# Full attention on one core: column scores issued head by head, and the order of a step's work on TensorE changed

## What is computed

```python
scores = jnp.einsum('bhqd,bhkd->bhqk', q, k) / np.float32(np.sqrt(HD))
attn = jax.nn.softmax(scores, axis=-1)
out = jnp.einsum('bhqk,bhkd->bhqd', attn, v)
```

## Time and profile before

| | us |
|---|---|
| median of 3 runs | 4614.77 (4614.61 to 4633.34) |
| profiled execution | 4615.12 |
| its span in the profile | 4613.0 |
| PE busy | 4186.8 (91%) |
| DVE busy | 3628.9 (79%) |
| ACT busy | 2805.2 (61%) |
| mean granted share of the full PE clock | 0.962 |

### The profile page before, as it was taken

How to read it: one execution, slowest core, us unless ns; L and a number is a source line. 1 busy time by engine, 2 the same in 40 slices (tenths; PEclk the granted TensorE clock), 3 DMA queues, 4 the chain that set the end, 5 groups by cost and what they waited for, 6 DMA issues and landing times. The chain is left out here.

```text
span 4613.0 us, 82689 instructions
## 1 busy us (share of the span) xinstructions
PE 4186.8 (91%) x27418; PEld 2681.1 (58%) x27418; DVE 3628.9 (79%) x8000; ACT 2805.2 (61%) x6209; POOL 1631.0 (35%) x2408
## 2 busy tenths in 40 slices
PE   5959999999999976599999996999799999987998
PEld 2523333333333334377777775888577777766887
DVE  6679999999999949688888884555688888875665
ACT  1428888888888860366767673444467676763343
POOL 2400000000000004465555653444465656554555
PEclk8969999999999998799999997999899999998999
DMA  5943243333343317300000001211200000003221
GB/s 193 374 88 58 48 63 57 49 63 56 49 63 57 49 61 238 100 27 24 27 24 27 24 19 55 57 47 42 60 24 27 24 27 24 27 13 87 84 69 54
DMA packets 368556, 295.67 MB, mean 64 GB/s; under 512 B 66364, under 2 KB 325432, under 8 KB 368192
## 3 DMA queue, kind: packets, MB, share of 16 engines
q1 hardware_dynamic: 368192, 291.11, 25.6%
HBM read 178.74 MB, written 111.21 MB: 63 GB/s over the span
## 5 line engine op out<-in xcount | busy, mean ns | idle before, releaser
L885 ACT ACTIVATE fa_P<-fa_pS 128x512 f32<-128x512 f32 x2048 | 1111.7, 595 | 317.0 <-PE fa_pS L811 267.2
L912 DVE TENSOR_REDUCE fa_mx<-fa_pR 128x2 f32<-128x1024 f32 x1024 | 1206.0, 1221 | 92.6 <-PE fa_pR L792 78.3
L1507 POOL TENSOR_TENSOR wa_pn<-wa_pr,wa_ri 128x512 f32<-128x512 f32 x512 | 700.7, 1369 | 521.7 <-DVE wa_ri L1563 520.8
L1443 ACT ACTIVATE wa_pr<-wa_sm,wa_mn 128x256 f32<-128x256 f32 x1024 | 510.6, 502 | 172.2 <-DVE wa_mn L1555 172.2
L1136 POOL TENSOR_TENSOR ao_xn<-ao_xn,ao_mod 128x1024 f32<-128x1024 f32 x16 | 37.5, 2347 | 1585.9 <-DVE ao_xn L1101 1585.9
L826 PE MATMUL fa_pO<-fa_P,fa_V 128*32 128x512 f32 x4096 | 546.4, 605 | 0.2 <-ACT fa_P L885 0.2
L811 PE MATMUL fa_pS<-fa_Q,fa_K 50*128 50x512 f32 x2048 | 507.5, 492 | 41.3 <-ACT fa_P L885 11.0
L811 PEld LDWEIGHTS fa_pS<-fa_Q,fa_K 50*128 50x128 f32 x2048 | 191.2, 183 | 517.1 <-ACT fa_P L885 431.3
L792 PE MATMUL fa_pR<-fa_K,fa_Q 48*128 48x512 f32 x2048 | 430.7, 463 | 57.3 <-DMA fa_K<-parts_d 38.3
L1295 PE MATMUL wa_pQK<-wa_wqkv,wa_xT 128*128 128x512 f32 x1536 | 420.0, 409 | 4.7 <-DVE wa_qa L1600 4.7
L1555 DVE CUSTOM_DVE_ANT_0 wa_sm<-wa_pS,wa_mask 128x256 f32<-128x256 f32 x1024 | 374.1, 420 | 18.5 <-issue 11.6
(11 more groups left out here) (188 smaller groups left out, 7156.6 us busy)
## 6 DMA issues: line engine op xcount, KB each, us to landing
parts_d<-pj_parts SPq DMA_DIRECT2D x64, 512.0 KB, 5.4
fa_Q<-parts_d SPq DMA_DIRECT2D x192, 128.0 KB, 4.4
fa_K<-parts_d SPq DMA_DIRECT2D x192, 128.0 KB, 7.4
v_d<-pj_v SPq DMA_DIRECT2D x16, 1024.0 KB, 8.2
fa_V<-v_d SPq DMA_DIRECT2D x32, 512.0 KB, 9.7
pj_x<-in_L_attn_x SPq DMA_DIRECT2D x16, 512.0 KB, 7.6
fa_Q<-fa_nrow SPq DMA_DIRECT2D x512, 2.0 KB
att_d<-fa_att SPq DMA_DIRECT2D x64, 128.0 KB, 2.0
```

The source lines that it names most:

```text
L885: nc.scalar.activation(Pr[:, k % 2, h, :], pS[:, (s * exped.per + u) % T, :], ACT.Exp).then_inc(exped.sem, 1)
L912: nc.vector.tensor_reduce(mx[:, q // QB, :, a, q % QB, kh], row_slot(), AX.X, ALU.max).then_inc(row_free, 1)
L1443: last = nc.scalar.activation(pr[:, hp % 2, hh, :], sm[:, hp % 2, hh, :], ACT.Exp, bias=mn[:, p, h:h + 1], scale=-1.0, accum_out=rs[:, p, ...
L1507: nc.gpsimd.tensor_tensor(pn[:, hp % 2], pr[:, hp % 2], inv, ALU.mult).then_inc(s["weighted"].sem, 1)
```

## The change

`scores` takes a head instead of a pair. It issues one matmul and has a wait of its own, on the exponential three heads earlier. The steps of TensorE's `body` are in another order: head 0, head 1, first row pair, head 2, value batch of the step before, head 3, second row pair, and then the turn where there is one. The number of matmuls, their shapes, the three banks and the two slots stay as they were. TensorE has two more waits for each step.

```diff
-                def scores(n, s, k, a):
+                def scores(n, s, k, h):
                     half, kb = k // KB, k % KB
-                    u = k * GH + 2 * a
-                    if kb == 0 and a == 0:
+                    u, a, at = k * GH + h, h // 2, h % 2 * TOP
+                    if kb == 0 and h == 0:
                         pe.wait_ge(max_in[half].sems[s], max_in[half].upto(n))
-                    if not (is_first(n) and u < 2):
-                        pe.wait_ge(exped.sem, n * exped.per + u - 1)
-                    for e in range(2):
-                        at = e * TOP
-                        nc.tensor.matmul(pS[:, (s * exped.per + u + e) % T, :],
...
+                    if not (is_first(n) and u < T):
+                        pe.wait_ge(exped.sem, n * exped.per + u - T + 1)
+                    nc.tensor.matmul(pS[:, (s * exped.per + u) % T, :],
...
                     for k in range(STEPS):
                         scores(n, s, k, 0)
+                        scores(n, s, k, 1)
                         if not is_last(n):
                             row_scores(n + 1, (s + 1) % NB, 2 * k)
-                            row_scores(n + 1, (s + 1) % NB, 2 * k + 1)
-                        scores(n, s, k, 1)
+                        scores(n, s, k, 2)
                         if k > 0:
                             sums(n, s, k - 1)
                         elif not is_first(n):
                             sums(n - 1, (s - 1) % NB, STEPS - 1)
+                        scores(n, s, k, 3)
+                        if not is_last(n):
+                            row_scores(n + 1, (s + 1) % NB, 2 * k + 1)
                         if k == 0:
                             turn_max(n, 1)
```

## The result

The changed kernel takes 4704.66 us (median of 4 runs, 4701.11 to 4714.87), the kernel before 4614.69. The ratio is 1.0184, with a 95% interval of 1.0167 to 1.0201. The forecast was 4704 in a range of 4682 to 4728. The profiled execution took 4701.11, with a span of 4699.0, which is 86.0 longer than before.

What follows compares the result with a forecast made beforehand. The prediction took a loop of waits through one exponential and the value batch, 2.61 us per plain step, as the bound. Longer turn steps, summed over the groups, added 89.1 to the profiled 4615.1: 4704, range 4682 to 4728.

Steps and rivals of the forecast that it cites:

- The plain step stays at 2.61: Step without a turn: the new loop has the same five terms, 2.62 by rounded rows, taken as 2.61 again.
- rival of a ring that gives overlap: At the score banks: head 2 not tied to the value batch's exponential, loop 0.43 shorter; about 4540; chance 0.02.
- The turn step gets 1.12 longer: Steps with a turn: the next first row pair waits for the second pair's slot, adding 1.12 to the step.
- The turn fits into the wait: Behind the second row pair: the turn loads at about 2.10 or 2.33, within the slot's wait; both kinds cost 1.12.
- Heads with their own waits cost nothing: Two more waits per step: costed at nothing, hidden by 0.2 us of slack, up to 0.02 each if not.
- rival of loads that aren't hidden: On TensorE: a lone matmul with its own wait loads only after the one before, 0.34 per link; 4796; chance 0.07.
- The sum: Whole stage: group 0 +2.4, groups 1 to 30 +87.0, last group -1.2 and +0.9 at its end; together 89.1.
- The bounds: Turn steps' 1.12 could be 1.06 to 1.19, -7 to +9 us; plain steps 0.01 to 0.02 off, 4 to 8.
- Hidden turns: At the turns: they would lie between head 3 and head 2, their old cost mostly vanishing; 4565; chance 0.04.
- It changes nothing: Whole kernel: the moved waits are all met anyway, so the time stays 4615; chance 0.02.
- signs that were named: Steps 1, 3, 9, 11: first row pair waits for DVE, TensorE idle 0.3 to 0.9; steps 3.73, groups 46.2 apart.

Runs made afterwards that it cites:

- e6: Changed kernel with the second row pair directly behind the value batch, ahead of head 3; 4776 us (one run).
- e9: Changed kernel with each exponential over half of its queries, the value batch reading the first half twice; 4643 us (one run).
- e2: Changed kernel with the turn ahead of the second row pair, on TensorE and VectorE; ratio 1.0061 to the kernel before.
- e4: Changed kernel with each row pair's reduction over half of its columns and exponentials scaled by 0.01; 4623 us (one run).
- e1: Kernel before with heads issued singly, each with its own wait, in the old order; ratio 0.9994 to the kernel before.
- e5: Changed kernel with the second row pair and head 3 moved ahead of the value batch; ratio 0.9992 to the kernel before.
- e3: Changed kernel with the turn directly behind the value batch, ahead of head 3, second row pair last; ratio 1.0009 to the kernel before.
- e7: Changed kernel with the value batch over half of the queries, the copy reading the first half twice; 5060.6 us (one run).
- e8: Kernel before with each row pair's reduction over half of its columns and exponentials scaled by 0.01; 4622 us (one run).

## Why the prediction was right, step by step

- **The plain step stays at 2.61.** Right: 969.67 - 967.06 = 2.61 in the kernel after. e6 shows that the stretch from value batch to head 3 is on the loop. e9 lost 0.22 of a step for 0.215 of each exponential, so one is on it. That head 2 hangs on the same exponential as the value batch is read from the code and agrees with these; no run changed the number of banks, so the rival of a ring that gives overlap is refuted by the step of 2.61 alone.
- **The turn step gets 1.12 longer.** Right in mechanism, 0.02 too long in size (3.73 forecast, 3.71 measured). Its terms, forecast and measured in the stretch shown above: value batch to head 3, 1.00 and 0.99 (964.36 - 963.37); head 3's load to the start of the second pair's reduction, 0.50 + 0.24 + 0.05 = 0.79 and 965.12 - 964.36 = 0.76; the reduction and its signal, 1.27 and 966.40 - 965.12 = 1.28; first pair's load to the value batch, 0.50 + 0.24 - 0.07 = 0.67 and 0.66. The term that came out smaller is the second.
- **The turn fits into the wait.** Right: the `turn_sums` loads 965.01 - 962.94 = 2.07 behind head 2 (2.10 forecast), heads 0 and 1 at 2.66 (2.69). Hence both kinds end up at the same length, and e2 and e4 moved them as the slot's time says.
- **Heads with their own waits cost nothing.** Right, shown by e1. In the kernel after the neighbours even overlap across kinds: head 3 and the second pair load together at 964.36, and the pair's end comes 0.24 behind head 3's. The rival of loads that aren't hidden falls with that. The Trainium skill ("TensorE: Matmul & The Clock Gate", Part 3, what overlaps and what doesn't) says that a weight load overlaps running matmuls only where its row group differs. The trace of the kernel after disagrees, as that of the kernel before did: head 0's weights load at 968.16, while the second pair's first matmul, on the same rows, runs from 968.06 to 968.56 by its modelled end:

```profile
968.06 0.50 PE L792 MATMUL fa_pR<-fa_K,fa_Q 48*128 48x512 f32 x1
968.16 0.19 PEld L809 LDWEIGHTS fa_pS<-fa_Q,fa_K 50*128 50x128 f32 x1
```

  The alternation of row groups brought no gain here, in e5 either, though a step that is set by the loop would hardly show one.
- **The sum.** Counted from the start of each group's first score matmul, group 0 gave 2.7 more us than before (2.4 forecast; the granted clock also rose later in it, 0.50 from 317.1 to 321.2 where it was 1.00 before), groups 1 to 30 gave 30 x (46.12 - 43.285) = 85.1 (87.0 forecast), the last group, up to its last value batch, -0.5 (-0.3 forecast). The stage's first scores came 0.5 later (308.1 against 307.6), so it ended 87.9 later, at 1782.89 for the last value batch against 1694.97. The rest of the program then took 1.9 less than before. Why, no run shows. The forecast of 89.1 on the profiled execution was thus 3 us too long. That the median of the runs came out within 1 us of 4704 is in part luck: it lies 3.5 above the profiled execution. The bounds and one rival count 124 turn steps, one too many, since group 0 has three; that shifts them by about 0.1 to 0.2 us.
- **The other rivals.** *Hidden turns* had a true core. In the last group, which has no row pairs, the moved turn costs 2.68 - 2.61 = 0.07 in place of 0.58. In the other groups the slot's wait is for the second pair, as forecast, and the turns don't hide. I had left open what else would be needed. e5 has the reduction early, but it also puts head 3 ahead of the value batch and so the turns on the loop, where they cost 0.2 and 0.58 as before; it doesn't test an early reduction with the turn behind head 3. *It changes nothing* falls with the measured 86 us.
- **The signs that were named came out.** TensorE's weight loads are idle 0.62 and 0.78 ahead of the first pair, inside the 0.3 to 0.9 given, and the brackets name `fa_mx`. The brackets also name ACT on heads 0 and 1 after a turn, where ACT had long been done, so that name is to be passed over.

## What to carry to other kernels

Where two buffers rotate among a regular use and a rare one, count in the steps with the rare use which instruction has to be consumed for the next one, and when that one is issued. A pair of matmuls moved from the start of a step to its end was free in twelve steps of sixteen here and on the path in the other four. The place that holds the rare use counts as much: behind head 3 it was all but free in the last group, and in e3, ahead of head 3, the rare uses cost nearly what they did before. Splitting a pair of instructions to give each its own wait gained nothing, since the loop of waits, with one producer, one consumer and the long batch between them, passed through the same instructions as before.

## What the runs showed of the hardware that was not expected

- **With less work on TensorE its clock stayed down, in the one run of e7.** There the value batch was halved and the stage never left 0.50 (1.2 GHz): TensorE came to the stage at the lower clock, as it does in the kernel before (its matmuls of row pairs take 0.79 in the prologue and 0.40 to 0.50 later), but did not rise. In the kernel before the clock rose about 10 us after the first column scores, in the kernel after about 13 us after them. That the halved batch is the cause is not shown, since e7 ran once. The run is 360 us longer than that of the kernel after (5060.6 - 4701.1).
- **It dropped for a moment in e9** in about every third group, near the turn in step 8. The sums of the stretch itself, and in the second row of the one just before it:

```profile
1000.40:1003.80 3.40, 3.40 (x17) 1.51 (x16) 1.42 (x2) 1.01 (x3) 0.00 (x0) 0.52 0.01 2
996.60:1000.40 3.80, 3.09 (x18) 1.02 (x17) 3.63 (x7) 2.01 (x6) 0.00 (x0) 1.00 0.64 142
```

  In the 3.8 us before, which hold the turn and the wait for the slot, TensorE was busy for 3.09; then the granted clock was 0.52 and a value batch took 1002.27 - 1000.43 = 1.84 instead of 1.00. Each such group is 1.3 us longer.
- **In e6 and e8 it fell in the last group**, where there are no row pairs, and plain steps took 4.07 there; in the kernels before and after the same group ran at 1.00. The sums of the last group shown at the top of the result have 1.00, and the earlier trace rows has it for the kernel before. What decides between these cases the runs don't show.
